# A four-layer graph network: each tile of edges gathered once per aggregation, its ring slot read from a register, dense stages between the last steps

## What is computed

```
edge_index = stack([src, dst])                      # dst is sorted
for each of four blocks: h = relu(layernorm(x)); x = x + block(h)
block 0, three layers:  z = relu(segment_sum((z @ W)[src] * norm, dst) + b),  norm = dis[src]*ew*dis[dst]
                        (the edge list has a self-loop for each node: dis[n]*dis[n])
block 1:  relu((h + segment_sum(ew * h[src], dst)) @ G1 + c1) @ G2 + c2
block 2:  attention over the edges (segment softmax by dst), then a dense layer
block 3:  normalised rows of  mean_by_dst(h[src]) @ Wl.T + bl + h @ Wr.T
```

## Time and profile before

| | |
|---|---|
| median of 3 runs | 7518.55 us (7517.9 to 7519.48) |
| the profiled execution | 7519.79 us, with a span of 7518.0 us between first and last instruction |
| busy, of the span | PE 76%, DVE 51%, ACT 16%, POOL 67% |
| mean granted TensorE clock | 0.969 |
| instructions | 99962 |
| gathers of the passes | 4160 indirect DMAs on POOL |

### The profile page before, as it was taken

The page is one execution under the profiler, slowest core; times in us unless marked ns, Lnnn a source line. Parts: engine busy times, 40 slices in busy tenths (PEclk is TensorE's granted clock), DMA queues, the critical chain, the costliest instruction groups (busy, mean ns, idle before and its releaser), DMA issues.

```text
span 7518.0 us, 99962 instructions
## 1 busy us (share of the span) xinstructions
PE 5718.0 (76%) x30467; PEld 3476.1 (46%) x30467; DVE 3806.6 (51%) x12655; ACT 1181.4 (16%) x3122; POOL 5039.7 (67%) x5069
## 2 busy tenths in 40 slices
PE   0677777777777777777577777899999995677776
PEld 0444444444444444444344444455555553444444
DVE  8834444444444444444544444577777777433335
ACT  0600000000000000000100000466666664000000
POOL 7077777677777677777577776466666661677774
PEclk9599999999999999999899999999999997999999
DMA  1021111211111211111111111354555450111111
GB/s 49 20 62 53 53 53 53 60 53 53 53 53 53 60 54 53 53 53 53 55 53 53 53 53 48 100 124 120 124 125 122 122 124 20 55 53 53 53 53 51
DMA packets 393953, 491.18 MB, mean 65 GB/s; under 512 B 104941, under 2 KB 291215, under 8 KB 393403
## 3 DMA queue, kind: packets, MB, share of 16 engines
q0 software_dynamic: 160528, 330.23, 15.7%
q1 hardware_dynamic: 229723, 153.27, 8.2%
q10 hardware_dynamic: 3168, 1.31, 0.1%
HBM read 459.92 MB, written 26.88 MB: 65 GB/s over the span
## 4 chain that ended last, share of the span: by engine, by line
POOL 52%; PE 22%; issue 17%; DVE 6%; ACT 1%; DMA 1%; ACTq 0%; DVEq 0%; POOLq 0%; SPq 0%
POOL pool L623 52%; PE psum L790 8%; PE psum L813 3%; PE psum L779 3%; PE psum L772 2%; DVE pool L1217 2%; PE psum L656 1%; PE psum L765 1%; PE psum L758 1%; PE psum L801 1%; PE psum L736 1%; PE psum L722 0%; DVE hot L1309 0%; DVE work L1051 0%; ACT work L929 0%
## 5 line engine op out<-in xcount | busy, mean ns | idle before, releaser
L623 POOL DMA_INDIRECT pool<-table,src_col x4160 | 3933.6, 946 | 1440.4 <-issue 1265.9
L745 PE MATMUL psum<-busy_rows,iota_b 128*128 128x512 bf16 x12480 | 3393.0, 381 | 0.0
L747 PE MATMUL psum<-pool 128*128 128x128 f32 x8320 | 1714.3, 288 | 1380.4 <-DVE pool L1342 1380.4
L747 PEld LDWEIGHTS psum<-pool 128*128 128x128 f32 x8320 | 1503.7, 191 | 2346.8 <-DVE pool L1342 1894.2
L1342 DVE TENSOR_SCALAR pool<-iota_f,rel_col,ew_col 128x128 f32<-128x128 f32 x3328 | 1228.5, 374 | 2291.4 <-DMA pool<-table,src_col 2290.4
L745 PEld LDWEIGHTS psum<-busy_rows,iota_b 128*128 128x128 bf16 x12480 | 1235.2, 99 | 545.9 <-issue 9.0
L1353 DVE TENSOR_TENSOR work<-work,psum 128x128 f32 x4160 | 1190.1, 286 | 252.6 <-PE psum L747 224.2
L605 POOL DMA_INDIRECT gath<-table,src_col x832 | 909.4, 1093 | 535.7 <-PE psum L765 341.2
L942 ACT ACTIVATE pool<-psum 128x512 f32<-128x512 f32 (+1 forms) x130 | 72.1, 566 | 4278.8 <-PE psum L722 4278.7
L790 PE MATMUL psum<-pool,head_sum 128*32 128x512 f32 x1248 | 614.9, 602 | 0.0
L1342 DVE TENSOR_SCALAR pool<-iota_f,rel_col 128x128 f32<-128x128 f32 x832 | 238.5, 287 | 577.6 <-DMA pool<-table,src_col 577.0
(11 more groups left out here) (195 smaller groups left out, 3938.6 us busy)
## 6 DMA issues: line engine op xcount, KB each, us to landing
pool<-table,src_col POOLq DMA_INDIRECT x4160, 2.5
pool<-edge_attr SPq DMA_DIRECT2D x832, 64.0 KB
pool<-step_masks SPq DMA_DIRECT2D x208, 192.0 KB
pool<-rel_rows SPq DMA_DIRECT2D x208, 128.0 KB, 3.1
table<-work SPq DMA_DIRECT2D x60, 256.0 KB, 2.3
gath<-table,src_col POOLq DMA_INDIRECT x832, 3.3
table<-QV SPq DMA_DIRECT2D x12, 256.0 KB, 2.3
out<-X SPq DMA_DIRECT2D x12, 256.0 KB
```

The source lines that it names most:

```text
L623: gp.indirect_dma_start(out=gath_ring[:, s % RING, :], out_offset=None, in_=source[:, :], in_offset=bass.IndirectOffsetOnAxis(ap=src_col[: ...
L745: pe.matmul(psum[:, SUM_BANKS, :], iota_b[:, :], busy_rows[:, :], start=True, stop=True)
L747: pe.matmul(psum[:, s % SUM_BANKS, 0:D], hot_ring[:, s % HOT_RING, :], gath_ring[:, s % RING, :], start=True, stop=True).then_inc(steps.pr ...
```

## The change

Five things are done together.

1. **One gather per tile.** `gathers` runs over the 782 tiles, not over 832 steps. `src_col` holds the sources by tile. A new plan row gives each step its tile modulo 64; PE loads 16 of these at a time into registers and reads the slot of `gath_ring` by register. Steps 782 to 829 have no gather of their own, and steps 830 and 831 are no longer done (`PS` = 830). Since step s may use a tile as old as s - 48, gather t now waits until step t - 13 is multiplied, checked at every `FREE` = 4th tile.
2. **Dense stages between the last 48 steps.** `products` takes a list of stages and does one after every fourth step from 782 + 6 on; `sums` calls a function for a group after every fourth step from 782 + 14 on (`DRAIN_AT`), or 782 + 6 (`STAGE_AT`) behind pass 2. A group is taken as complete when `NT` + last block of it - 1 steps or more are added. In these steps PE does no extra matmuls, and the products go to four banks (7, 6, 2, 3), in pass 4 to two (7, 6), so that the dense stage has the others.
3. **Node factor and bias.** The add takes the factor of its block (`dis`, in pass 4 `inv_cnt`) with it, as a scalar_tensor_tensor with both block and factor by register. The biases b0 and b1 go into ACT's relu, b2 into one tensor_tensor per group, and POOL multiplies `Y` by `dis` where it copied. `bias_add` and `mean` are gone.
4. `KEEP_BUSY` is 2, not 3.
5. **Sources twice.** The sources by step, which attention needs, are turned too (two more groups in `COLS`), both forms are stored in DRAM, and SP loads `src_col` by step after pass 3 and by tile after attention.

```diff
-        BATCH = 4
-        FREE = 8
+        BATCH = 4
+        FREE = 4
...
-        KEEP_BUSY = 3
+        KEEP_BUSY = 2
...
-                for arr, dest in ((rel, rel_col), (ew_f, ew_col), (srcf, src_col), (endr, end_col))
+                for arr, dest in ((rel, rel_col), (ew_f, ew_col), (tile_src, src_col), (endr, end_col), (srcf, step_src))
...
+            def slot_free(self, t):
+
+                steps = t + FREE - 1 - RING + NB - 1 + 1
+                return self.nth * (PS // FREE) + ceil_div(steps, FREE) if steps > 0 else 0
+
+            def bank(self, s):
+                return s % SUM_BANKS if s < NT else self.tail_banks[(s - NT) % len(self.tail_banks)]
+
+            def lead(self, s):
+
+                return (SUM_BANKS if s < NT else len(self.tail_banks)) - 1
+
+            def group_added(self, g):
+
+                return self.before + NT + groups[g][1] - 1
...
-                    gp.tensor_copy(AGG[:, lo:hi, :], Y[:, lo:hi, :]).then_inc(gcn_started, 1)
+                    gp.tensor_tensor(AGG[:, lo:hi, :], Y[:, lo:hi, :], col_bc(dis, lo, hi), ALU.mult).then_inc(gcn_started, 1)
...
-            for s in range(NS):
-                if s % FREE == 0 and s >= RING:
-                    gp.wait_ge(steps.freed, (steps.before + s - RING) // FREE + 1)
+            for t in range(NT):
+                if t % FREE == 0 and t >= RING - NB:
+                    gp.wait_ge(steps.freed, steps.slot_free(t))
...
+            def stage_at(k):
+                if k < NGR:
+                    turn(k)
+                if k >= 1:
+                    multiply(k - 1)
...
-            for s in range(NS):
-                for _ in range(KEEP_BUSY):
-                    pe.matmul(psum[:, SUM_BANKS, :], iota_b[:, :], busy_rows[:, :], start=True, stop=True)
+            for s in range(PS):
+                if s % REGS == 0:
+                    slots = load_plan(mybir.EngineType.PE, 2, s, REGS, RING - 1, "the plan takes the tile modulo RING")
+                if s < NT:
+                    for _ in range(KEEP_BUSY):
+                        pe.matmul(psum[:, SUM_BANKS, :], iota_b[:, :], busy_rows[:, :], start=True, stop=True)
                 pe.wait_ge(steps.hot, steps.before + s + 1)
-                pe.matmul(psum[:, s % SUM_BANKS, 0:D], hot_ring[:, s % HOT_RING, :], gath_ring[:, s % RING, :], start=True,
+                pe.matmul(psum[:, steps.bank(s), 0:D], hot_ring[:, s % HOT_RING, :],
+                          gath_ring[:, bass.ds(slots[s % REGS], 1), :].rearrange("p a d -> p (a d)"), start=True,
                           stop=True).then_inc(steps.product(s)[0], 1)
+                if then and s >= NT + STAGE_AT and (s - NT - STAGE_AT) % GROUP == 0:
+                    then.pop(0)()
+            for stage_of in then:
+                stage_of()
...
-                act.activation(tr[:, b, 0:n * P], psum[:, b, 0:n * P], func).then_inc(d.copied, 1)
+                act.activation(tr[:, b, 0:n * P], psum[:, b, 0:n * P], func, bias=bias).then_inc(d.copied, 1)
...
+            def gcn_drain(layer, g):
+                lo, hi = groups[g]
+                v.wait_ge(gcn[layer].multiplied, gcn[layer].before + g + 1)
+                v.tensor_tensor(Y[:, lo:hi, :], product_of(g), col_bc(dis, lo, hi), ALU.mult).then_inc(gcn[layer].drained, 1)
+
+            def gcn_out(g):
+                lo, hi = groups[g]
+                v.wait_ge(passes[2].added, passes[2].group_added(g))
+                v.tensor_tensor(AGG[:, lo:hi, :], AGG[:, lo:hi, :], bias_of("b2", hi - lo), ALU.add).then_inc(own.up(), 1)
...
+            for s in range(PS + SUM_BANKS):
+                while added < PS and (s >= PS or added < s - steps.lead(s)):
+                    if added % REGS == 0:
+                        blocks = load_blocks(mybir.EngineType.DVE, added, REGS)
+                    v.wait_ge(*steps.product(added))
+                    if added >= 1:
+                        v.wait_ge(steps.added, steps.before + added)
...
+                        v.scalar_tensor_tensor(into, part, scale[:, bass.ds(blocks[added % REGS], 1)], into, ALU.mult,
+                                               ALU.add).then_inc(steps.added, 1)
+                    added += 1
+                if s < PS:
+                    if s < NT and s % BATCH == 0:
+                        v.wait_ge(batch_here[s // BATCH % NBATCH], batch_value(steps.nth, s))
...
+                    if s >= NT + then_at and (s - NT - then_at) % GROUP == 0:
+                        then(groups_done)
+                        groups_done += 1
+            for g in range(groups_done, NGR):
+                then(g)
```

More of the change, by code:

```diff
@@ L355, in build, with batch_value, tiles_to @@
         gin_1, gin_2, q_dense, v_dense, o_dense, sage_dense = (Dense(3 + i) for i in range(6))
[L356 to L361 removed]
+        passes = [Pass(i, (7, 6, 2, 3)) for i in range(4)] + [Pass(4, (7, 6))]
+        batch_here = [sem(f"batch_here{i}") for i in range(NBATCH)]
+        def batch_value(nth, t):
+            of_sem = t // BATCH % NBATCH
+            def tiles_to(end):
+                return sum(min(BATCH, NT - lo) for lo in range(of_sem * BATCH, end, RING))
+            return 16 * (nth * tiles_to(NT) + tiles_to(t + 1))
         qsrc_here = [sem(f"qsrc_here{i}") for i in range(SLOTS)]
         gcn_started = sem("gcn_started")
[L366 removed]
         stored = [sem(f"stored{i}") for i in range(6)]
@@ L930, in normalise, with dense_copies @@
             ins.then_inc(norm.normed, 1)
-        def dense_copies(act, d, K, func, after=None):
+        def dense_copies(act, d, K, func, after=None, bias=0.0):
             def copy(g):
@@ L1117, in vector @@
             settle()
-            sums(v, 4, passes[4], False)
-            def mean(g):
-                lo, hi = groups[g]
-                if g == 0:
-                    v.wait_ge(passes[4].added, passes[4].before + NS)
-                v.tensor_tensor(AGG[:, lo:hi, :], AGG[:, lo:hi, :], col_bc(inv_cnt, lo, hi), ALU.mult).then_inc(mean_made, 1)
             def result(g):
@@ L1135, in result, with sage_drain @@
                 v.tensor_tensor(X[:, lo:hi, :], X[:, lo:hi, :], st, ALU.add).then_inc(result_made, 1)
-            mean(0)
-            mean(1)
-            for g, (lo, hi) in enumerate(groups):
+            def sage_drain(g):
+                lo, hi = groups[g]
                 n = hi - lo
@@ L1154, in vector @@
                     result(g - 1)
-            result(NGR - 1)
+                if g == NGR - 1:
+                    result(g)
+            sums(v, passes[4], None, inv_cnt, DRAIN_AT, sage_drain)
         def product_of(g):
@@ L1333, in norm_feed, with sums @@
                 norm_end(v, norm, g)
[L1335 removed]
+        def sums(v, steps, weight, scale, then_at, then):
             v.wait_ge(plan_loaded, 16)
[L1338 to L1354 removed]
```

188 lines of the change are left out of this document (103 added, 85 removed).

## The result

The changed kernel took 7307.16 us (median of 4 runs, 7305.54 to 7308.04), the kernel before 7518.9 us (7517.9 to 7519.48). The ratio is 0.9718, 95% interval 0.9701 to 0.9735: 2.8% faster, with 7307 forecast. The profiled execution took 7305.5 us, its span 7303.8 against 7518.0 before, 214.2 less.

What follows compares the result with a forecast made beforehand. POOL's gathers were taken to bound the passes, DVE and PE the gaps between. Net terms -44.4 - 46.9 - 42.3 - 46.9 - 35.1 + 4 = -211.6 us gave 7307 us, 2.8% faster; range 7270 to 7395.

Steps and rivals of the forecast that it cites:

- What bounds the kernel: Inside a pass only POOL's gathers count, 1.2504 us each; between passes DVE and PE set the end.
- The common tail: Last 48 steps of every pass, without POOL: start, pairs at 0.50 us, lagging adds and register loads, 33.5 us.
- Pass 0 and 1: Gap behind each: common tail, nine drains, port hold and end make 54.1 us; net -44.4 and -46.9 us.
- the hold: Tails of passes 0 and 1: POOL's multiplication, 1.3 us, stops DVE's one-hot behind each drain; 9 x 1.0 = 9.0 us.
- Pass 2: Gap behind it: common tail plus DVE's output work, 76.9 us against 56.7 before; net -42.3 us.
- Pass 4: End of the kernel: two banks, pairs of about 0.70 us; 97.7 us from the last gather; net -35.1 us.
- The start: Ahead of pass 0: one more array of columns, a cast and POOL's multiplications add 4 us.
- the clock: Rival: fewer extra matmuls lower PE's clock, which reaches the tails; 74 us more, 7382 us. Chance 0.16.
- The case without a hold: Rival: one-hots slip past POOL, which multiplies at the copy's price; passes 0 and 1 -12 us, 7285 us. Chance 0.15.
- PE as the pace: Rival: low clock and register cost make PE the pace of whole passes; 938 us more, 8246 us. Chance 0.05.
- the short window: Rival: gathers stop for slots, POOL waiting at every fourth tile; gain gone at 54 ns a gather, 7519 us. Chance 0.02.
- the third rival: PE becomes the pace of the whole pass: clock at 1.2 GHz plus register cost; 8246 us at x = 0.21. Chance 0.05.

Runs made afterwards that it cites:

- e5: The changed kernel unaltered, run again as a control on a chip of the 7519 us kind: 7312.48 us, ratio 0.9722.
- e7: The changed kernel with all dense stages and their drains moved behind the last step of each pass: 7331.44 us.
- e9: The changed kernel with ACT in place of POOL starting the next sum (Y times dis), on a slower chip: 8099.19 us.
- e10: The changed kernel with the node factors dis and inv_cnt left out of the adds, on a slower chip: 8090.95 us.
- e8: As e7, and the last 48 steps of each pass left out with their products and adds: 7176.45 us.
- e12: The changed kernel unaltered, run again as a control on a slower chip: 8106.58 us, ratio 0.9446.
- e6: The changed kernel with no extra matmuls ahead of the products (KEEP_BUSY 0 in place of 2): 7311.43 us.
- run 49: Not a run label: in "in the first run 49 did", 49 counts adds that waited over 0.5 us; the first run is the changed kernel, 7307.16 us.

## Why the prediction was right, and where its terms were off

**What bounds the kernel**: right. Gathers stood 1.249 to 1.253 us apart in the five passes, in the first run and in e5; POOL waits 0.30 us, and where its releaser is a product (132 waits, 40.2 us in all) the pace is the same. The window has room, on a chip of that kind.

**The common tail, 33.5 us**: two terms were off. I took the scalar_tensor_tensor at the price of the tensor_tensor, "the idle 0.21 behind it is there anyway". That step failed: its 0.35 us stand in the chain with 0.24 of wait, so a pair is 0.585, and 57 of them are 4.9 us more. On the other side I added the whole 0.84 us of each register load to a pair that already held a wait; three loads cost 3 x (0.80 - 0.24) = 1.7, not 2.5. The sum would have been 37.5; in e7, where nothing stands among the steps, the last add of pass 0 ended 38.0 us behind the last gather. Pass 3 still has a tensor_tensor and 0.50; PE's first transposes of `gin_2` stand at 4525.59 us, 42.1 behind the last gather for 41.9 forecast.

**Pass 0 and 1, 54.1 for 53.95 and 54.35**: right in part by luck, since errors cancel. The pairs are +4.9; the hold is 9 x 0.63 = 5.7 in place of 9.0, since POOL's instruction took 1.04 us, between my bounds of 0.65 and 2.06 but below the 1.3 that I took; a drain costs 0.53 and not 0.68, 1.4 less. Together +0.2, and the register loads take 0.8 off. That the hold costs all of 5.7 us is read from the rows; e9, without it, gave back 4.7 and 4.1. The Trainium skill's GPSIMD Engine Reference (section 3.1) has 4497 ns for 2048 columns; in plain proportion, an estimate from that page, 512 columns take 1.12 us, which is nearer than mine and than the 1.2 that I made of it. The end was right: from the end of the last add (1412.38 + 0.35) to the first gather lie 5.6 us, forecast 5.5.

**Pass 2, 76.9 for 82.45**: the one gap that is off by much, and nearly all of it is the factor. With 4.9 for the pairs it is 81.8, and e10 took 4.9 of it away again; the last 0.6 us (1.4 with the register loads at their true price) is not accounted for. It is also the tail in which interleaving has nothing to give (e7: 81.26).

**Pass 4, 97.7 for 96.7**: the sum was right, its split not. A step costs 0.84 us (e8), not 0.70; on the other side the stages among the steps return 8.5 us (e7), which I had at 0 except for their waits. Two rows from its steps show DVE waiting for PE's product:

```profile
7217.35 0.35 DVE L1430 SCALAR_TENSOR_TENSOR work<-psum,inv_cnt,work 128x128 f32 x1 [0.86 <-PE psum L825]
...
7229.40 0.35 DVE L1430 SCALAR_TENSOR_TENSOR work<-psum,inv_cnt,work 128x128 f32 x1 [3.81 <-PE psum L825]
```

Before the first groups every other add waits 0.5 to 0.9 us for its product, and behind the two early stages an add waited 1.59 and 3.81: 4.4 us over the usual 0.52, for which I had 4.0.

**The start, +4 for +0.4**: mis-sized. The first gather of pass 0 went from 388.12 to 388.54; in e5 it came at 390.21, in e12 at 388.18, so the start costs 0 to 2 us. That the added arrays of columns and the cast lie beside other work is an inference; beside which, I did not look into. `gin_2` to pass 4 is 4.0 us shorter without a forecast; of the same stretch e5 had 1708.0 us, e6 1704.6 and e7 1708.4, so it is within what a run varies by, and no part of the change is shown to do it.

**The rivals**: the clock is out by e6. The case without a hold is out by 1.03 us one-hots. PE as the pace and the short window did not happen on chips of the 7519 kind. On the others POOL did stop for slots, for a cause that neither names: the last section.

## What to carry to other kernels

When the bounding engine loses work, price what comes out at its pace and the tail that it leaves at the pace of the next engine; the gain is the difference (312 us of gathers gave 214). In a chain of dependent adds the price of a step is the add plus the wait for it (0.585 us, with or without a one-hot between), so only what lengthens the add or stands in the chain counts: a factor in the add cost 0.085 a step, the one-hot nothing. Before interleaving, look for work that needs nothing of the tail and put it where the engine idles, as the bias (8.65 us for moving 13 instructions, on the slower kind of chip); the interleaving itself gave 19 us.

## What the runs showed of the hardware that was not expected

Two of the three chips of the experiments ran the kernels 11 to 14% slower (before: 8587 and 8581 us against 7519; changed: 8107 against 7312). In a waits view of the changed kernel on such a chip (e12; us in total, times, longest):

```profile
POOL pool L684 <- issue: 1092.5, 3585, 0.3
POOL pool L684 <- remote: 889.2, 320, 3.6
...
DVE work L1430 <- remote: 1345.6, 365, 6.5
DVE work L1430 <- PE psum L825: 699.7, 379, 3.5
DVE pool L1436 <- DMA pool<-table,src_col: 638.6, 336, 10.4
```

and of the first run of the changed kernel:

```profile
DVE pool L1436 <- DMA pool<-table,src_col: 2448.4, 978, 10.3
...
DVE work L1430 <- PE psum L825: 163.1, 212, 3.8
```

Most gathers stood 1.25 us apart there too, but 64 times a pass POOL stopped for 2.8 us or so, waiting for a slot that a product frees, while DVE waited up to 6.5 us for a product. The time was not lost at the transfers: DVE waited 639 us for gathered rows, where in the first run it was 2448. Nor was PE short of time. From e12, PE's products and DVE's adds in pass 0, in order of time:

```profile
682.76 0.63 PE L825 MATMUL psum<-pool 128*128 x2
684.04 0.42 PE L825 MATMUL psum<-pool 128*128 x2
...
687.33 0.39 PE L825 MATMUL psum<-pool 128*128 x2
689.46 0.35 DVE L1430 SCALAR_TENSOR_TENSOR work<-psum,dis,work 128x128 f32 x1 [3.54 <-PE psum L825]
690.22 0.48 PE L825 MATMUL psum<-pool 128*128 x2 [2.07 <-DVE pool L1436]
692.67 0.35 DVE L1430 SCALAR_TENSOR_TENSOR work<-psum,dis,work 128x128 f32 x1 [2.61 <-remote]
```

Counted from the start of the pass, the adds at 689.46 and 692.67 take the products that begin at 682.76 and 684.04, so they came 6.7 and 8.6 us after these had begun. PE had begun five more products by 687.33, and then stood idle for 2.07 us until DVE made the next one-hot, which in DVE's order comes behind the waiting add. In that pass of e12, 206 of the 782 adds outside the tail waited over 0.5 us, 549 us in all; in the first run 49 did, 40 us in all, each behind a register load. So what came late was the word that a product is done, and not PE's turn to do it. Whether the array ended late or only its signal did can't be told, since the profile models the ends of matmuls.

A third extra matmul made it worse (1.462 us a gather against 1.452). So on such a chip the steps and not POOL's instructions were the pace, as in the third rival, but not by that rival's sum of a low clock and a register. The change still gained there, 5.5%: PE's steps fell only from 832 to 830 a pass, so the fewer gathers alone don't explain that. What holds the products' ends back there, and why the kernel before loses more (1062 to 1068 us against 794), is open: the granted clock was lower (0.80 against 0.88), but e6 shows that a clock at 0.50 in the passes costs nothing on a chip of the other kind. A kernel without extras on such a chip would tell more, and was not run.
